# Transposing the first-occurrence counts by DMA from ScalarE's queue, and a select product behind each s product

## The chip, the cores and the metric

One core of a Trainium2 chip. The metric is the device time of one launch in microseconds (us); lower is better. Engines: TensorE (PE), VectorE (DVE), ScalarE (ACT), GpSimd (POOL), and SyncE (SP), which issues all the transfers of the kernel before. TensorE's granted clock was 0.999 of its upper level (2.4 GHz) over the whole profiled execution.

## The reference, cut to what matters

Two layers run on x of shape 4 x 512 x 512 (four chunks of 512 rows). Each layer is `xn = layernorm(x); x = x + s(xn) * silu(g(xn))`. The change touches layer 0's g:

```
inter = xn @ c1_w.T @ c2_w.T                       # [rows, 1792], rank 16
blk   = inter.reshape(rows, 56, 32)                # 56 segments of 32
idx   = argmax(blk, axis=-1) + arange(0, 1792, 32) # first largest in each segment
h     = relu(sum(w1[idx] * xn))                    # one h for each segment
g     = h @ w2t[idx]
```

and layer 0's s is `xn @ (block-masked weight).T + bias`. The kernel computes g densely: h for all 1792 columns, set to zero where the column isn't the first largest of its segment, and then times w2t.

## The kernel before, in words

Float32 products are done as three products of a high and a low part (`three`, L372 to L377), so PE does most of its work in one helper line, L376. Layer 0 handles one chunk after another. A chunk has a head and a body, on PE, DVE and ACT alike.

**Head.** `rank_product` (8 products) gives t, which ACT (L710) and DVE (L901) split. Then come four s products of 12 matmuls each, one for each tile of 128 rows; they alternate between banks 0 and 1, and ACT empties a bank with `s_read` (L716), so that s product tt waits for s_read tt-2. The 1792 columns of `inter` are cut into four pieces, p = 0 to 3 (512, 512, 512 and 256 columns), and each piece has four row tiles tt. For one pair (p, tt), PE computes a select product (L1182) into bank 6, and DVE does three steps, `select`: the largest of each segment (L914, seg_top), equality with it (L916, eq), and a scan that restarts at each segment and counts the equals so far (L926, counts). The row tiles of piece 0 are done in the head, with PE's select tt one s product late: s0, s1, select 0, s2, select 1, s3, select 2; select 3 follows the first up product.

**Body.** `it` runs over the 14 tiles of 128 columns. PE: up product `it` (12 matmuls, h transposed: columns on partitions), one select product of the next piece while it <= 12, `transpose_counts(it - 1)`, and the down product `it - 2` (12 matmuls into banks 2 to 5). `transpose_counts` is four transposes of 128x128 bf16 (L1201) of counts into bank 7, because counts has rows on partitions and h has columns there. ACT: relu of the up product into h (L728; waits for h_lo of the tile before), then h_hi (L737). DVE: a `select` of the next piece, the mask h = (count is 1) * h (L944, reads bank 7), and h_lo (L953). The down product `it` waits for h_lo `it`. Only one relu'd h exists at a time. A new chunk's rows are normalized and transposed at the end of the body (L354, L314, L321, L328).

Counts has room for two pieces of four row tiles. Before its first use, its bytes serve as `c2_rep`, a zeroed tile (L861) in which ACT spreads c2_w (L756) for PE to transpose.

**Startup.** PE, ACT and DVE turn the weights (`items`: PE transposes, ACT `item_hi`, DVE `item_lo`), three items after each s product of chunk 0 (`AFTER_S`). An item's bank is free when item n-5 is split (`w_lo`). The mask of w_s0 goes DVE L884, PE L1258, DVE L889, POOL L639. POOL then splits w2 and later adds the bias and gates.

**SP** issues the loads in its own order; in a chunk it loads the next x_tile and then x_res (1 MB each) once the stores of the chunk before have landed.

Of the kernel before, what the change touches and what calls it, by code (L numbers as in the profile page):

```python
# [6 lines left out]
P = 128  # L7
# [11 lines left out]
def block_mask_ffn_then_attention_lora_kernel(  # L19
# [53 lines left out]
    with ctx:  # L73
# [52 lines left out]
        c1_stack = span_c.take("c1_stack", [P, KD, P], F32R)  # L126
        c1_nat = span_c.take("c1_nat", [RANK, D])
        next_c = Span(span_c.start)
        wqkv_nat = next_c.take("wqkv_nat", [P, KD, 3 * DH])
# [4 lines left out]

        span_s = Span(max(span_c.end, next_c.end, next_c2.end))
        ws_hi = span_s.take("ws_hi", [P, KD, D], F32R)
# [36 lines left out]
        h_lo = span_2.take("h_lo", [P, 2, S], F32R)  # L173
        mask_nat = before_h.take("mask_nat", [P, TT, D], I32)
        rest_2 = Span(span_2.start)
# [45 lines left out]
        mask_on = sem("mask_on")  # L221
        ws0_masked = sem("ws0_masked")
        c2_wide = sem("c2_wide")
        half_bias = sem("half_bias")
# [18 lines left out]
        sel_count = sem("sel_count")  # L243
        first_tr = sem("first_tr")
        up_done = sem("up_done")
# [138 lines left out]
        c2_nat = x_res[:, 0, 0:IT * RANK].rearrange("p (i r) -> p i r", r=RANK)  # L384
        c2_rep = counts[:].bitcast(F32).rearrange("p a t n -> p (a t n)")[:, 0:IT * P]
        c2_rep_q = c2_rep.rearrange("p (i q r) -> p i q r", q=4, r=Q)
# [3 lines left out]
        mask_bank = banks[5]  # L390
        first = banks[7][:].bitcast(BF16)[:, 0:S]
        NSEL = PIECES * TT
# [103 lines left out]
        def item_hi(act, n):  # L496

            kind, i = items[n]
            act.wait_ge(w_tr, n + 1)
            if kind == "c1":  # L500
                act.wait_ge(consts_dve, 12)
# [203 lines left out]
        def _(act):  # L705
# [6 lines left out]
            def s_read(c, tt):  # L712
# [39 lines left out]

            act.wait_ge(consts_dve, 12)
            act.wait_ge(ld_c2, 16)
# [101 lines left out]
        def _(dve):  # L856
# [7 lines left out]
            dve.wait_ge(consts_dve, 6)  # L864
            nc.vector.memset(restart[:].rearrange("p (s n) -> p s n", n=SEG)[:, :, 0:1], 0.0).then_inc(consts_dve, 1)
# [54 lines left out]
            def select_count(c, p, tt):  # L920
                n = p * TT + tt
                dve.wait_ge(sel_eq, c * NSEL + n + 1)
                if tt == 0 and p >= 2:

                    dve.wait_ge(first_tr, c * IT + 4 * (p - 1))
                nc.vector.tensor_tensor_scan(counts[:, p % 2, tt, 0:PW[p]], restart[:, 0:PW[p]], eq[:, 0:PW[p]], 0.0,  # L926
                                             ALU.mult, ALU.add).then_inc(sel_count, 1)

            def head(c):
                t_rest(c)  # L930
                for tt in range(TT - 1):
                    select(c, 0, tt)

            def body(c, last):
                select(c, 0, TT - 1)
                for it in range(IT):
# [39 lines left out]
            for tt in range(TT):  # L976
                if tt:
                    select(0, 0, tt - 1)
                for n in AFTER_S[tt]:
                    item_lo(dve, n)  # L980
            with dve.Fori(0, CH - 1) as c:
                body(c, False)
# [173 lines left out]
        def _(pe):  # L1156
# [37 lines left out]

            def transpose_counts(c, it):

                pe.wait_ge(sel_count, c * NSEL + (it // 4 + 1) * TT)
                if it:
                    pe.wait_ge(h_masked, c * IT + it)
                for tt in range(TT):  # L1200
                    last = nc.tensor.transpose(first[:, rows(tt)], counts[:, it // 4 % 2, tt, rows(it % 4)], ident_bf[:])  # L1201
                last.then_inc(first_tr, 1)

            def down_product(it, tts):
# [7 lines left out]
            def head(c):  # L1212
                pe.wait_ge(xT_done, c * TT + TT)
                rank_product()
                s_product(c, 0)
                s_product(c, 1)
                select(c, 0, 0)
                s_product(c, 2)
                select(c, 0, 1)
                s_product(c, 3)  # L1220
                select(c, 0, 2)

            def body(c, last):
                up_product(c, 0)
                select(c, 0, 3)


                for it in range(1, IT + 1):
# [10 lines left out]
                    transpose_counts(c, it - 1)  # L1239
                    if it >= 2:  # L1240
# [31 lines left out]
            for tt in range(TT):  # L1272
# [3 lines left out]
                for n in AFTER_S[tt]:  # L1276
                    item_in(pe, n)
            with pe.Fori(0, CH - 1) as c:
                body(c, False)
# [192 lines left out]
```

## Time and profile before

| | us |
|---|---|
| median of three runs | 699.52 |
| lowest, highest | 699.08, 701.77 |
| profiled execution, first to last instruction (span) | 697.0 |
| chunk 1 of layer 0, from one rank product to the next (131.36 to 233.53) | 102.2 |
| layer 1 begins at about | 430 |

The profiled execution has no separate total on the page, only its span; the median stands 2.5 us above it, and that difference is what lies around the instructions. Rows of a timeline give start and duration in us, then engine, line, operation, the tile written and the tile read; in square brackets stands the idle time of the engine just before and what ended it. "Issue" rows of SPq are the instructions that start a DMA. Matmul ends are modelled: the distance between starts tells what a product costs.

### The profile page before, as it was taken

What the parts mean: (1) busy time and instruction counts of PE and PEld (TensorE: products, weight loads), DVE (VectorE), ACT (ScalarE), POOL (GpSimd) and SP (SyncE); (2) the same over time, 40 slices, a digit from 0 to 9 for tenths busy, and PEclk for the clock granted to TensorE, in tenths of its full rate; (3) what the DMA queues carried; (4) which work ended last, traced back from release to release, by engine and by line L of the source; (5) the groups of instructions that cost most, each with busy time, mean ns of one, the idle gap of its engine ahead of it and who ended that gap; (6) DMA issues with size and microseconds to landing.
All of it is one profiled execution on the core that took longest, in us unless ns stands there. A gap on an engine that the chain in (4) does not pass through costs nothing.

```text
span 697.0 us, 9078 instructions
## 1 busy us (share of the span) xinstructions
PE 671.0 (96%) x3220; PEld 529.0 (76%) x3220; DVE 457.7 (66%) x741; ACT 208.3 (30%) x371; POOL 204.2 (29%) x175
## 2 busy tenths in 40 slices
PE   4989999999999999999999999889999999999997
PEld 3867777777777777787777787667877887787787
DVE  8798664596765596665686656684855566485543
ACT  2621222412122312222311132563136115313610
POOL 3299100360000550000630003624424242442441
PEclk9999999999999999999999999999999999999999
DMA  8563000040000040000150004530021013002001
GB/s 273 188 189 111 14 1 0 23 159 0 0 0 0 31 149 0 0 0 0 45 197 1 0 1 122 121 136 1 30 91 62 0 46 135 0 30 90 1 15 46
DMA packets 30570, 40.25 MB, mean 58 GB/s; under 512 B 11888, under 2 KB 12656, under 8 KB 30544
## 3 DMA queue, kind: packets, MB, share of 16 engines
q1 hardware_dynamic: 30544, 39.90, 17.5%
q8 instruction: 16, 0.26, 0.2%
q14 instruction: 10, 0.08, 0.0%
HBM read 31.51 MB, written 8.39 MB: 57 GB/s over the span
## 4 chain that ended last, share of the span: by engine, by line
PE 83%; DVE 9%; issue 4%; DMA 1%; ACT 1%; POOL 1%; SPq 0%; DVEq 0%; POOLq 0%
PE bank L376 73%; DVE eq L916 2%; DVE seg_top L914 2%; PE bank L1201 2%; PE bank L314 2%; DVE counts L926 2%; PE bank L1297 2%; DMA s_tile<-in_L_attn_weight 1%; PE bank L1182 1%; PE bank L1334 1%; PE bank L1162 1%; POOL s_tile L639 1%; DVE h_lo L953 1%; DVE w1T_lo L522 1%; DVE x_tile L354 0%
## 5 line engine op out<-in xcount | busy, mean ns | idle before, releaser
L737 ACT ACTIVATE h_hi<-h 128x512 fp32r<-128x512 f32 x56 | 35.4, 632 | 206.6 <-DVE h L944 206.6
L376 PE MATMUL bank<-w_hi_t,h_hi 128*128 128x512 f32 x224 | 93.6, 418 | 0.8 <-DVE h_lo L953 0.6
L914 DVE TENSOR_REDUCE seg_top<-bank 128x16 f32<-128x512 f32 (+1 forms) x64 | 39.5, 617 | 77.2 <-PE bank L1182 77.2
L376 PE MATMUL bank<-xT_hi,w1T_hi 128*128 128x512 f32 x224 | 88.7, 396 | 0.0
L376 PE MATMUL bank<-w_hi_t,h_lo 128*128 128x512 f32 x224 | 88.5, 395 | 0.0
L376 PE MATMUL bank<-w_lo_t,h_hi 128*128 128x512 f32 x224 | 88.5, 395 | 0.0
L376 PE MATMUL bank<-xT_hi,w1T_lo 128*128 128x512 f32 x224 | 88.5, 395 | 0.0
L376 PE MATMUL bank<-xT_lo,w1T_hi 128*128 128x512 f32 x224 | 88.4, 395 | 0.0
L926 DVE TENSOR_TENSOR_SCAN counts<-restart,eq 128x512 bf16<-128x512 bf16 (+1 forms) x64 | 82.1, 1283 | 2.0
L346 POOL TENSOR_TENSOR rstd<-mean_var,eps 128x4 f32<-128x4 f32 x8 | 1.6, 203 | 271.9 <-DVE mean_var L340 271.9
L360 POOL TENSOR_TENSOR g_tile<-g_tile,s_tile 128x512 f32<-128x512 f32 x31 | 40.6, 1311 | 104.9 <-DVE g_tile L970 66.1
L693 POOL TENSOR_TENSOR prod_lo<-prod,prod_hi 128x512 fp32r<-128x512 f32 x32 | 40.7, 1292 | 64.1 <-ACT prod_hi L782 63.9
L953 DVE TENSOR_TENSOR h_lo<-h,h_hi 128x512 fp32r<-128x512 f32 x56 | 41.3, 738 | 27.0 <-ACT h_hi L737 25.4
L376 PE MATMUL bank<-b_hi,prod_hi 128*128 128x512 f32 (+1 forms) x136 | 52.7, 387 | 0.0
L376 PE MATMUL bank<-b_hi,prod_lo 128*128 128x512 f32 (+1 forms) x136 | 51.4, 378 | 0.0
L376 PE MATMUL bank<-b_lo,prod_hi 128*128 128x512 f32 (+1 forms) x136 | 51.3, 377 | 0.0
L728 ACT ACTIVATE h<-bank 128x512 f32<-128x512 f32 x56 | 33.6, 599 | 57.5 <-DVE h_lo L953 48.0
L376 PEld LDWEIGHTS bank<-w_hi_t,h_lo 128*128 128x128 f32 x224 | 42.1, 188 | 10.1
L376 PEld LDWEIGHTS bank<-xT_hi,w1T_lo 128*128 128x128 f32 x224 | 42.0, 188 | 10.0
L376 PEld LDWEIGHTS bank<-xT_lo,w1T_hi 128*128 128x128 f32 x224 | 42.1, 188 | 9.9
L376 PEld LDWEIGHTS bank<-xT_hi,w1T_hi 128*128 128x128 f32 x224 | 42.1, 188 | 9.8
L376 PEld LDWEIGHTS bank<-w_hi_t,h_hi 128*128 128x128 f32 x224 | 42.2, 188 | 8.8 <-DVE h_lo L953 1.4
(201 smaller groups left out, 1327.4 us busy)
## 6 DMA issues: line engine op xcount, KB each, us to landing
x_res<-in_L_attn_data SPq DMA_DIRECT2D x4, 1024.0 KB, 7.6
mid_state<-g_tile SPq DMA_DIRECT2D x16, 256.0 KB, 2.1
x_tile<-mid_state SPq DMA_DIRECT2D x4, 1024.0 KB, 7.5
x_res<-mid_state SPq DMA_DIRECT2D x4, 1024.0 KB, 5.5
out<-g_tile SPq DMA_DIRECT2D x15, 256.0 KB, 2.0
x_tile<-in_L_attn_data SPq DMA_DIRECT2D x3, 1024.0 KB, 5.4
g_tile<-in_L_ffn_w SPq DMA_DIRECT2D x8, 256.0 KB, 5.4
g_tile<-in_L_ffn_w2t SPq DMA_DIRECT2D x8, 256.0 KB, 3.7
```

The costliest lines, as they stand in the source:

```text
L314: last = nc.tensor.transpose(rows_bank(g, tt)[:, k * P:(k + 1) * P], x_tile[:, tt, k * P:(k + 1) * P], ident[:])
L360: nc.gpsimd.tensor_tensor(g_tile[:, tt, :], g_tile[:, tt, :], s_tile[:, tt, :], ALU.mult).then_inc(s_free, 1)
L376: last = nc.tensor.matmul(dst, a, b, start=(start and n == 0), stop=(stop and n == len(mms) - 1))
L693: nc.gpsimd.tensor_tensor(prod_lo[:, kt, :], prod[:, kt % 3, :], prod_hi[:, kt, :].bitcast(F32), ALU.subtract).then_inc(prod_split, 1)
L728: nc.scalar.activation(h[:], up[it % 2][:], ACT.Relu).then_inc(relu_done, 1)
L737: nc.scalar.activation(h_hi[:, it % 2, :], h[:], ACT.Copy).then_inc(h_hi_done, 1)
L914: nc.vector.reduce_max(seg_top[:, 0:segs], got, AX.X).then_inc(seg_max, 1)
L916: nc.vector.tensor_tensor(eq[:, 0:PW[p]].rearrange("p (s n) -> p s n", n=SEG), got, seg_top[:, 0:segs, None].to_broadcast([P, segs, SEG]), ...
L926: nc.vector.tensor_tensor_scan(counts[:, p % 2, tt, 0:PW[p]], restart[:, 0:PW[p]], eq[:, 0:PW[p]], 0.0, ALU.mult, ALU.add).then_inc(sel_co ...
L953: nc.vector.tensor_tensor(h_lo[:, it % 2, :], h[:], h_hi[:, it % 2, :].bitcast(F32), ALU.subtract).then_inc(h_split, 1)
L1201: last = nc.tensor.transpose(first[:, rows(tt)], counts[:, it // 4 % 2, tt, rows(it % 4)], ident_bf[:])
L1297: nc.tensor.matmul(pj[kt % 2][:], pick[:, kt, :], combT[:], start=True, stop=True).then_inc(spread_done, 1)
```

## The change

- Counts are no longer transposed by PE. When a row tile's scan is done, ACT waits for it and issues a DMA transpose from SBUF to SBUF into a new tile `first` (two pieces), with all of the piece's columns at once (128 x 512 or 128 x 256 bf16). There are 16 such DMAs in a chunk. Each row tile has a semaphore for the landing.
- DVE's mask reads `first` instead of bank 7, and at the first tile of each piece waits for the four landings.
- `counts` shrinks to two row tiles. A scan waits until the transpose of the row tile two before has landed.
- ACT's transposes of piece 0 stand in the head behind each s_read; in chunk 0, that of tile tt-1 stands between s_read tt and the three items. In the body, one follows h_hi while it < 12.
- PE's select tt follows s product tt in the head, and select 3 comes before up product 0. DVE's four selects of piece 0 are all in the head.
- `c2_rep` moves onto mask_nat's bytes. So its memset goes from DVE's start to a place behind the wait for `mask_cnt`, ahead of L889.

```diff
-        counts = span_2.take("counts", [P, 2, TT, BANK], BF16)
+        first = span_2.take("first", [P, 2, TT, S], BF16)
...
+            def turn_counts(c, p, tt):
+                act.wait_ge(sel_count, c * NSEL + p * TT + tt + 1)
+                if p >= 2:
+                    act.wait_ge(h_masked, c * IT + 4 * (p - 1))
+                elif not (isinstance(c, int) and c == 0):
+                    act.wait_ge(h_masked, c * IT)
+                act.sem_inc(turns, 1)
+                act.dma_start_transpose(first[:, p % 2, 0:PW[p] // P, rows(tt)], counts[:, tt % 2, 0:PW[p]])\
+                    .then_inc(ld_first[tt], 16)
...
             def head(c):            # ACT
                 t_round(c)
                 for tt in range(TT):
                     s_read(c, tt)
+                    turn_counts(c, 0, tt)
...
                     nc.scalar.activation(h_hi[:, it % 2, :], h[:], ACT.Copy).then_inc(h_hi_done, 1)
+                    if it < 4 * (PIECES - 1):
+                        turn_counts(c, it // 4 + 1, it % 4)
...
             t_round(0)              # ACT, chunk 0
             for tt in range(TT):
                 s_read(0, tt)
+                if tt:
+                    turn_counts(0, 0, tt - 1)
                 for n in AFTER_S[tt]:
                     item_hi(act, n)
+            turn_counts(0, 0, TT - 1)
...
-            nc.vector.memset(c2_rep, 0.0).then_inc(consts_dve, 1)     # DVE's start
...
             dve.wait_ge(mask_cnt, 1)
+            nc.vector.memset(c2_rep, 0.0).then_inc(c2_zero, 1)
             nc.vector.tensor_scalar(on[:, 0:TT * MB], mask_bank[:, 0:TT * MB], 0.0, None, ALU.is_gt).then_inc(mask_on, 1)
...
-                if tt == 0 and p >= 2:
-                    dve.wait_ge(first_tr, c * IT + 4 * (p - 1))
+                turned = c * PIECES + p + (1 if tt >= 2 else 0)
+                if not (isinstance(turned, int) and turned == 0):
+                    dve.wait_ge(ld_first[(tt + 2) % TT], turned * 16)
...
-                    dve.wait_ge(first_tr, c * IT + it + 1)
-                    nc.vector.scalar_tensor_tensor(h[:], first, 1.0, h[:], ALU.is_equal, ALU.mult).then_inc(h_masked, 1)
+                    if it % 4 == 0:
+                        for tt in range(TT):
+                            dve.wait_ge(ld_first[tt], (c * PIECES + it // 4 + 1) * 16)
+                    nc.vector.scalar_tensor_tensor(h[:], first[:, it // 4 % 2, it % 4, :], 1.0, h[:], ALU.is_equal, ALU.mult).then_inc(h_masked, 1)
...
-            def transpose_counts(c, it):     # PE, and its call in the body
...
             def head(c):            # PE
                 pe.wait_ge(xT_done, c * TT + TT)
                 rank_product()
-                s_product(c, 0)
-                s_product(c, 1)
-                select(c, 0, 0)
-                s_product(c, 2)
-                select(c, 0, 1)
-                s_product(c, 3)
-                select(c, 0, 2)
+                for tt in range(TT):
+                    s_product(c, tt)
+                    select(c, 0, tt)
             def body(c, last):
                 up_product(c, 0)
-                select(c, 0, 3)
```

## Rows read from the trace of the kernel before

**Rows 1.** The page: busy time by engine; the chain that ended last, by engine.
```profile
PE 671.0 (96%) x3220; PEld 529.0 (76%) x3220; DVE 457.7 (66%) x741; ACT 208.3 (30%) x371; POOL 204.2 (29%) x175
...
PE 83%; DVE 9%; issue 4%; DMA 1%; ACT 1%; POOL 1%; SPq 0%; DVEq 0%; POOLq 0%
```

**Rows 2.** PE's timeline in one body iteration, from an up product on.
```profile
177.29 0.40 PE L376 MATMUL bank<-xT_hi,w1T_hi 128*128 128x512 f32 x1
...
180.33 0.40 PE L1201 MATMUL bank<-ident_bf,counts 128*128 128x128 bf16 x4
...
180.85 0.40 PE L376 MATMUL bank<-w_lo_t,h_hi 128*128 128x512 f32 x1
```

**Rows 3.** Timeline of ACT and DVE in the next iteration.
```profile
189.24 0.67 DVE L944 SCALAR_TENSOR_TENSOR h<-bank,h 128x512 f32<-128x512 bf16 x1
...
189.94 0.63 ACT L737 ACTIVATE h_hi<-h 128x512 fp32r<-128x512 f32 x1 [4.07 <-DVE h L944]
...
190.61 0.69 DVE L953 TENSOR_TENSOR h_lo<-h,h_hi 128x512 fp32r<-128x512 f32 x1
```

**Rows 4.** Timeline of chunk 1's head: DVE, and PE's first down product.
```profile
139.34 0.69 DVE L914 TENSOR_REDUCE seg_top<-bank 128x16 f32<-128x512 f32 x1 [4.12 <-PE bank L1182]
...
146.38 0.66 DVE L914 TENSOR_REDUCE seg_top<-bank 128x16 f32<-128x512 f32 x1
...
147.80 2.08 DVE L926 TENSOR_TENSOR_SCAN counts<-restart,eq 128x512 bf16<-128x512 bf16 x1
...
153.01 0.69 DVE L944 SCALAR_TENSOR_TENSOR h<-bank,h 128x512 f32<-128x512 bf16 x1 [0.56 <-PE bank L1201]
...
154.94 0.68 DVE L953 TENSOR_TENSOR h_lo<-h,h_hi 128x512 fp32r<-128x512 f32 x1
...
156.03 0.48 PE L376 MATMUL bank<-w_hi_t,h_hi 128*128 128x512 f32 x1
```

**Rows 5.** The page's DMA issues (KB each, us to landing), and an issue from SP's timeline.
```profile
b_nat<-in_L_ffn_B SPq DMA_DIRECT2D x4, 512.0 KB, 7.9
...
out<-g_tile SPq DMA_DIRECT2D x2, 128.0 KB, 1.7
a_nat<-in_L_ffn_A SPq DMA_DIRECT2D x1, 128.0 KB, 3.6
...
146.96 0.41 SPq L568 DMA_DIRECT2D x_tile<-in_L_attn_data  x1
```

**Rows 6.** All instructions on tile b_nat: its DMA issues, durations min/median/max in ns.
```profile
L586 SPq DMA_DIRECT2D b_nat<-in_L_ffn_B x4: 421/2254/4728, 428.2 to 435.6; - x4
```

**Rows 7.** Timeline of the end of chunk 1's body, each engine by itself.
```profile
216.60 0.40 PE L1201 MATMUL bank<-ident_bf,counts 128*128 128x128 bf16 x4
...
222.99 0.69 DVE L944 SCALAR_TENSOR_TENSOR h<-bank,h 128x512 f32<-128x512 bf16 x1 [2.61 <-PE bank L1201]
...
224.98 1.91 DVE L354 TENSOR_SCALAR x_tile<-x_tile,mean_var,rstd 128x512 f32<-128x512 f32 x4
...
219.02 0.63 ACT L737 ACTIVATE h_hi<-h 128x512 fp32r<-128x512 f32 x1 [3.88 <-DVE h L944]
```

**Rows 8.** Timeline of the startup: the memset, an issue, w_s0's mask.
```profile
2.34 1.55 DVE L861 MEMSET counts<- 128x1792 f32 x1 [0.32 <-issue]
...
5.51 0.69 SPq L552 DMA_DIRECT2D x_res<-in_L_ffn_c_w  x1
...
13.33 0.22 DVE L889 TENSOR_SCALAR h<-bank 128x64 f32<-128x64 f32 x1
...
13.79 4.33 POOL L639 TENSOR_TENSOR s_tile<-s_tile,h 128x512 f32<-128x512 f32 x4 [3.45 <-DMA s_tile<-in_L_attn_weight]
```

**Rows 9.** Timeline of chunk 0's head on DVE, from the first scan's end to the first mask.
```profile
33.51 1.26 DVE L522 TENSOR_TENSOR w1T_lo<-bank,w1T_hi 128x512 fp32r<-128x512 f32 x2
...
46.65 2.23 DVE L926 TENSOR_TENSOR_SCAN counts<-restart,eq 128x512 bf16<-128x512 bf16 x1
49.45 0.69 DVE L944 SCALAR_TENSOR_TENSOR h<-bank,h 128x512 f32<-128x512 bf16 x1 [0.57 <-PE bank L1201]
```

More of the change, by code:

```diff
@@ L127, in block_mask_ffn_then_attention_lora_kernel @@
         c1_nat = span_c.take("c1_nat", [RANK, D])
+        counts_at = Span(span_c.start + 4 * KD * 3 * DH)
+        counts = counts_at.take("counts", [P, 2, BANK], BF16)
         next_c = Span(span_c.start)
@@ L133, in block_mask_ffn_then_attention_lora_kernel @@
         prod = next_c2.take("prod", [P, 3, S])
-        span_s = Span(max(span_c.end, next_c.end, next_c2.end))
+        span_s = Span(max(span_c.end, counts_at.end, next_c.end, next_c2.end))
         ws_hi = span_s.take("ws_hi", [P, KD, D], F32R)
@@ L173, in block_mask_ffn_then_attention_lora_kernel @@
         h_lo = span_2.take("h_lo", [P, 2, S], F32R)
-        mask_nat = before_h.take("mask_nat", [P, TT, D], I32)
+        mask_nat = nc.alloc_sbuf_tensor_at("mask_nat", [P, TT, D], I32, offset=before_h.end)
+        c2_rep = before_h.take("c2_rep", [P, TT * D])[:, 0:IT * P]
         rest_2 = Span(span_2.start)
@@ L222, in block_mask_ffn_then_attention_lora_kernel @@
         ws0_masked = sem("ws0_masked")
+        c2_zero = sem("c2_zero")
         c2_wide = sem("c2_wide")
@@ L243, in block_mask_ffn_then_attention_lora_kernel @@
         sel_count = sem("sel_count")
-        first_tr = sem("first_tr")
+        turns = sem("turns")
+        ld_first = [sem(f"ld_first_{tt}") for tt in range(TT)]
         up_done = sem("up_done")
@@ L390, in block_mask_ffn_then_attention_lora_kernel @@
         mask_bank = banks[5]
-        first = banks[7][:].bitcast(BF16)[:, 0:S]
         NSEL = PIECES * TT
@@ L500, in item_hi @@
             if kind == "c1":
-                act.wait_ge(consts_dve, 12)
+                act.wait_ge(consts_dve, 11)
             if kind == "c2":
@@ L751, in _ @@
                 item_hi(act, n)
-            act.wait_ge(consts_dve, 12)
+            act.wait_ge(c2_zero, 1)
             act.wait_ge(ld_c2, 16)
@@ L860, in _ @@
             nc.vector.memset(c1_stack[:].bitcast(F32), 0.0).then_inc(consts_dve, 1)
-            nc.vector.memset(c2_rep, 0.0).then_inc(consts_dve, 1)
             nc.vector.memset(seg_ones, 0.0).then_inc(consts_dve, 1)
             nc.vector.memset(comb[:], 0.0).then_inc(consts_dve, 1)
-            dve.wait_ge(consts_dve, 6)
+            dve.wait_ge(consts_dve, 5)
             nc.vector.memset(restart[:].rearrange("p (s n) -> p s n", n=SEG)[:, :, 0:1], 0.0).then_inc(consts_dve, 1)
@@ L922, in select_count @@
                 dve.wait_ge(sel_eq, c * NSEL + n + 1)
-                if tt == 0 and p >= 2:
-                    dve.wait_ge(first_tr, c * IT + 4 * (p - 1))
-                nc.vector.tensor_tensor_scan(counts[:, p % 2, tt, 0:PW[p]], restart[:, 0:PW[p]], eq[:, 0:PW[p]], 0.0,
+                turned = c * PIECES + p + (1 if tt >= 2 else 0)
+                if not (isinstance(turned, int) and turned == 0):
+                    dve.wait_ge(ld_first[(tt + 2) % TT], turned * 16)
+                nc.vector.tensor_tensor_scan(counts[:, tt % 2, 0:PW[p]], restart[:, 0:PW[p]], eq[:, 0:PW[p]], 0.0,
                                              ALU.mult, ALU.add).then_inc(sel_count, 1)
@@ L930, in head @@
                 t_rest(c)
-                for tt in range(TT - 1):
+                for tt in range(TT):
                     select(c, 0, tt)
             def body(c, last):
-                select(c, 0, TT - 1)
                 for it in range(IT):
@@ L980, in _ @@
                     item_lo(dve, n)
+            select(0, 0, TT - 1)
             with dve.Fori(0, CH - 1) as c:
@@ L1193, in up_product @@
                                       for k in range(KD)]).then_inc(up_done, 1)
-            def transpose_counts(c, it):
[L1197 to L1202, printed above, removed]
             def down_product(it, tts):
@@ L1214, in head @@
                 rank_product()
-                s_product(c, 0)
-                s_product(c, 1)
-                select(c, 0, 0)
-                s_product(c, 2)
-                select(c, 0, 1)
-                s_product(c, 3)
-                select(c, 0, 2)
+                for tt in range(TT):
+                    s_product(c, tt)
+                    select(c, 0, tt)
             def body(c, last):
                 up_product(c, 0)
-                select(c, 0, 3)
                 for it in range(1, IT + 1):
@@ L1238, in body @@
                         transpose_rows(pe, c + 1, 0)
-                    transpose_counts(c, it - 1)
                     if it >= 2:
@@ L1277, in _ @@
                     item_in(pe, n)
+            select(0, 0, TT - 1)
             with pe.Fori(0, CH - 1) as c:
```

1 line of the change is left out of this document (removed).

## The prediction, made before the changed kernel ran

> **What bounds the kernel now.** I read the page first: PE is busy for 96% of the span and makes up 83% of the chain that ended last, DVE 9% [rows 1]. So a PE instruction that goes is worth its whole time wherever PE runs without a gap, and every wait that the change adds matters only where PE ends up waiting for it. Then PE's timeline of one body iteration [rows 2]: from 177.29 to 180.33 PE starts 12 up products and one select product, 0.234 us each, then the four transposes, and the second down product starts at 180.85. The 0.52 us between the last two hold one product (0.234), so the transposes cost 0.29. An iteration is 25 x 0.234 + 0.29 = 6.13 us. Third, ACT and DVE in the next iteration [rows 3]: mask, h_hi and h_lo end at 191.30, and PE's next down product comes at 180.54 + 2 x 6.13 = 192.80, so this chain has 1.5 us to spare. Last come the three places where PE does not run freely: a chunk's head, where DVE's selects end late and PE waits for h_lo [rows 4]; the end of the body [rows 7]; and the startup [rows 8, 9].
>
> **Transposes off PE (gain).** 14 groups in a chunk. Two stand before the first down product, whose start is set by DVE in any case, so 12 count: 12 x 0.29 = 3.5 us in each chunk, 14.0 in four. An iteration becomes 5.84. DVE's mask no longer waits for bank 7.
>
> **The two unknown prices.** No DMA transpose stands in the trace. First x, the time for which its issue holds ACT. Plain issues on SP took 0.41 [rows 5] and 0.69 [rows 8]; the slowest typical one, with its queue full, 2.25 [rows 6]. The transpose is the more complicated form, so I take 0.7, and 0.41 and 2.25 for the ends. Then L, from the issue to the landing of 128 KB. A plain store of 128 KB alone took 1.7, a load of 128 KB amid others 3.6, and 512 KB in runs of 256 bytes, queued, 7.9 [rows 5]. A chunk's head has SP's two loads of 1 MB beside it (one issued at 146.96), so I lean on 3.6 and add the 0.3 by which my x exceeds a plain issue: L = 3.9, ends 1.7 and 7.9. At the end of a body the piece has 256 columns, half the bytes. Between 3.6 for 128 KB and 7.9 for 512 KB lie 1.1 us per 100 KB, so 64 KB less is 0.7: 3.2 there.
>
> ACT itself has room: it idles 4.07 us before each h_hi [rows 3], and x fits there. The three masks in mid-body that wait for a new piece do not bind either: the last issue follows h_hi at 190.57, the next tile's mask is due at 189.24 + 5.84 = 195.08, which hides 4.5 us, and the spare 1.5 - 0.29 = 1.2 makes it 5.7. If L is above that, each such mask costs the excess.
>
> On the issue, the Trainium skill (DMA: Bandwidth & Descriptors, the table in the section on why a DMA increments its semaphore by 16) gives for earlier generations 631 cycles for a small transpose and, from SBUF to SBUF, one command per tile, 262,144 cycles for 8,192 tiles. [...] No row here shows it.
>
> **Chunk heads 1 to 3.** Before, DVE waits until 139.34 for select 0 (idle 4.12), then runs its selects without a gap [rows 4]. Select 0 now comes one s product earlier, 12 x 0.234 = 2.8 us, and all four follow: the fourth seg_top starts at 147.0 instead of 149.8. Its scan starts 1.42 later (146.38 to 147.80), at 148.4. The one before took 2.08 beside POOL's additions, which now cover the fourth too: it ends at 150.5. The landing is at 150.5 + L, the mask starts there, and h_lo ends 2.6 later, as from 153.01 to 155.62 before. PE's first down product starts at 153.15 + L against 156.03: a gain of 2.9 - L, with L = 3.9 a loss of 1.0. The waits of scans 2 and 3 for the landing of the tile two before are covered up to about L = 4.7 (scan 0 ends near 140.3, scan 2 starts near 145.0). s_reads now stand behind a wait for a scan: s product 3 and up products 0 and 1 wait for them, and relu 0 stands behind the fourth issue. PE has products left to do until h_lo, so for x up to about 1.5 this ends before the landing does: nothing.
>
> **End of each body.** The last piece's fourth transpose is issued behind h_hi 11. In the old trace this h_hi ended at 219.65, 3.05 after the transposes of that iteration [rows 7]; PE then has 3 x 12 products, 8.4 us, until the row transposes. These need the mask of tile 12, and then the first of four normalizations: 224.98 + 0.48 - 222.99 = 2.5 us after the mask starts. So PE waits for 3.05 + L + 2.5 - 8.4 = L - 2.85; before, this mask waited 2.6 us for PE instead. With 3.2: 0.4 us, in four chunks 1.6. This wait is what is late next once PE is faster.
>
> **Startup and chunk 0.** The memset of 1.55 us ran at 2.34, while loads were on their way [rows 8]. Now it stands ahead of L889 (13.33), on which POOL's masking of w_s0 waits (13.79), and the items, the s products and all else behind it: +1.5. Then the items: ACT's item_hi now waits for the scan of DVE and an issue, while DVE's item_lo before started at 33.51, right as its scan ended [rows 9]. DVE is without a gap from there to the first mask, so each of the three groups adds x + 0.6 for the copy + 0.1 for semaphores = 1.4: +4.2. Finally the mask: it began 0.57 after the last scan's end (46.65 + 2.23 = 48.88, 49.45), now L: +3.3. Chunk 0: 1.5 + 4.2 + 3.3 - 3.5 = +5.5. Here the cover is gone altogether, since DVE sets the pace.
>
> **Sum.** Chunk 0 +5.5; chunks 1 to 3: 3 x (1.0 - 3.5) = -7.5; ends +1.6: -0.4. Layer 1 has no change. From the span of 697.0 to 696.6, and with the 2.5 us around it, 699.1.
>
> **Rivals.** (1) The transposes are cheap: L = 2.2, x = 0.5. Head: -0.7 - 3.5 = -4.2 each; ends 0; chunk 0: 1.5 + 3.6 + 1.6 - 3.5 = +3.2. Sum -9.4: 690. For it speaks the store of 1.7 [rows 5] and idle DMA engines for most of the body; against it the two big loads in the head. The Trainium skill says as much (Advanced Engine Details and Errata, X-Bar Transpose (TRN2)): transposing DMAs are as fast as regular ones. With that rule the time would be this rival's.
>
> (2) Slower, because the landing is late at every place where PE waits for it: L = 5.5 in the heads and 5.0 at the ends, x = 1.2. Heads 5.5 - 2.9 + 0.8 for the scans that now wait - 3.5 = -0.1 each; ends 2.15 x 4 = +8.6; chunk 0: 1.5 + 5.7 + 4.9 - 3.5 = +8.6. Sum +17: 716. It decides from about L = 4.5 on. The load in small runs speaks for it, x_tile and x_res in the same engines too. The Trainium skill's rule that SP's and ACT's DMAs interleave on the same 16 engines (DMA: Bandwidth & Descriptors, Issuing engines are not separate DMA queues) points the same way.
>
> (3) L at 7.9 or over: the head +5 and some 6 for the scans' waits, three masks at 2.2 each, the end +4.4: some +18 per chunk after the 3.5 are off, about 770. Only the queued load speaks for it.
>
> (4) The issue holds ACT for 2.25, L = 4: chunk 0 1.5 + 8.9 + 3.4 - 3.5 = +10.3, heads 1.1 + 0.7 (up product 1 behind the last s_read) - 3.5 = -1.7 each; ends +1.8: +7, 706.
>
> (5) The change does less than it says: ACT's waits are met early and the ladder of chunk 0 hides, so that only the 14 us and the memset count: 687 to 690. DVE's timeline without a gap speaks against it.
>
> **How the numbers follow.** What a measurement of this kernel can tell from no change is about 0.5%, 3.5 us. The forecast 0.33, rival 1 0.25, rival 2 0.24, rival 3 0.07, rival 4 0.07, rival 5 0.04. Faster is rivals 1 and 5 and the lower edge of the forecast's own range: 0.31. Slower is rivals 2, 3, 4: 0.38. Same 0.31. The forecast alone spans 694 to 704. Each us of L costs 8 (three heads, the mask of chunk 0, four ends) and each us of x 3. With both at their low ends (1.7, 0.41) the sum is -11.7: heads -4.7 each, chunk 0 +2.4. The range takes in rival 1's 690 and rival 2's 716: 689 to 719.
>
> **What would show it.** PE without L1201, and iterations of 5.84 us. DVE's mask at a chunk's first tile idle and released by the DMA, 3 to 4 us after the last scan. PE's first down product released by h_lo, at about 157 on the old clock where it was 156.03. Row transposes of the next chunk waiting for DVE L354. POOL's L639 at 15.3. DVE idle about 1.4 us before each of three item groups. I'd be wrong if the landing took under 2.5 or over 5 us, or if PE lost time in mid-body.

## The result, and the profile after

The changed kernel takes 717.96 us (median of 5 runs, 714.30 to 719.22), the kernel before 700.21 beside it: a ratio of 1.0244, 95% interval 1.0217 to 1.0271. It is 17.75 us slower, where no change was forecast. The profiled execution has a span of 712.5 us against 697.0, so 15.5 of this stand in its trace. It is the fastest of the five; the others have spans of 716.0 to 717.4 us and granted clocks of 0.978 to 0.981 where it has 0.984, and there is no trace of them.

The page of the changed kernel: PE's busy time, the chain by engine, the mask's group (with its idle time and what ended it), and the queue of the transposes (packets, MB, share of 16 engines).

```profile
PE 666.9 (94%) x2996; PEld 526.6 (74%) x2996; DVE 460.5 (65%) x741; ACT 207.9 (29%) x371; POOL 205.8 (29%) x175
...
q10 hardware_dynamic: 30720, 7.35, 5.1%
...
PE 77%; DVE 11%; DMA 4%; issue 4%; ACT 2%; ACTq 1%; SPq 0%; DVEq 0%
...
L965 DVE SCALAR_TENSOR_TENSOR h<-first,h 128x512 f32<-128x512 bf16 x56 | 38.9, 694 | 28.2 <-DMA first<-counts 28.2
```

Against [rows 1], PE is busy for only 4.1 us less, though its transposes are gone, and its share fell from 96 to 94%. The DMA part of the chain went from 1% to 4%, 3% of it on tile `first`. DVE's mask now idles 28.2 us in all, all of it for the transposes' landing. 30,720 packets for 64 transposes are 480 each on average, of some 240 bytes.

All transposes by their line: durations of the issue in ns, and the time to landing.

```profile
L729 ACTq DMA_TRANSPOSE first<-counts x64: 1184/1206/1320, 36.1 to 437.9; - x64
...
DMA to landing us min/median/max: 2.3/2.4/8.0
```

So x, the time for which an issue holds ACT, is 1.21 us, and L, from issue to landing, is 2.4 in the median, but 8.0 at most. Where the long ones stand decides everything. The windows from one rank product to the next, chunks 1 and 2, and chunk 3 up to layer 1's first product (the row of a window: length, busy time and instructions of PE, PEld, DVE, ACT and POOL, then PE's clock, the DMA share and GB/s):

```profile
139.91:243.53 103.62, 99.36 (x425) 78.49 (x425) 68.62 (x97) 24.45 (x41) 19.76 (x14) 0.98 0.18 48
243.53:345.85 102.32, 98.38 (x425) 77.46 (x425) 68.64 (x97) 24.45 (x41) 19.84 (x14) 1.00 0.17 49
345.85:455.40 109.55, 101.81 (x428) 80.28 (x429) 73.02 (x99) 26.13 (x43) 24.63 (x18) 0.95 0.34 86
```

Before, these were 102.17, 102.14 and 104.43 long. The differences add up: chunk 0 with the startup +8.55 (chunk 1's rank product starts at 139.91, before at 131.36), then +1.45, +0.18, +5.12: +15.3 at the start of layer 1. The forecast had chunks 1 to 3 shorter by 2.5 each, with 0.4 given back at each end.

Mid-body, PE, from down product to down product (against [rows 2]):

```profile
175.69 0.39 PE L381 MATMUL bank<-w_hi_t,h_hi 128*128 128x512 f32 x1
...
181.51 0.39 PE L381 MATMUL bank<-w_hi_t,h_hi 128*128 128x512 f32 x1
```

5.82 us for 25 products without a gap, against 6.13: the gain in the body is there. It is lost in the head. DVE, ACT, SP and PE in chunk 1's head, each engine's timeline by itself:

```profile
157.13 2.06 DVE L946 TENSOR_TENSOR_SCAN counts<-restart,eq 128x512 bf16<-128x512 bf16 x1
165.97 0.69 DVE L965 SCALAR_TENSOR_TENSOR h<-first,h 128x512 f32<-128x512 bf16 x1 [6.78 <-DMA first<-counts]
...
167.30 0.69 DVE L936 TENSOR_TENSOR eq<-bank,seg_top 128x512 bf16<-128x512 f32 x1
167.91 0.68 DVE L974 TENSOR_TENSOR h_lo<-h,h_hi 128x512 fp32r<-128x512 f32 x1
...
155.91 1.21 ACTq L729 DMA_TRANSPOSE first<-counts  x1
...
159.31 1.32 ACTq L729 DMA_TRANSPOSE first<-counts  x1
...
156.40 0.41 SPq L571 DMA_DIRECT2D x_tile<-in_L_attn_data  x1
157.04 0.40 SPq L576 DMA_DIRECT2D x_res<-in_L_attn_data  x1
...
168.04 0.79 PE L1204 MATMUL bank<-c_stack,t_stack 128*128 128x512 f32 x1 [3.25 <-DVE eq L936]
168.64 0.79 PE L381 MATMUL bank<-w_hi_t,h_hi 128*128 128x512 f32 x1
...
170.51 0.63 PE L381 MATMUL bank<-w_lo_t,h_hi 128*128 128x512 f32 x1
170.94 0.48 PE L381 MATMUL bank<-w_hi_t,h_lo 128*128 128x512 f32 x1
171.26 0.39 PE L381 MATMUL bank<-w_hi_t,h_hi 128*128 128x512 f32 x1
```

The reader is to see three things against [rows 4]. The fourth scan ends at 159.19, 19.3 us after the chunk's rank product, where it was 21.1 before: the new order works. The transpose issued at 159.31 lands only at 165.85, beside two loads of 1 MB that were issued 2.9 and 2.3 us ahead of it (that these make it late is shown by the first two experiments). And after PE's wait of 3.25 us its products start 0.43 us apart instead of 0.233, which is the clock's lower level (1.2 GHz), until 171.26. From 168.64 on, six products take 2.62 us instead of 1.40, which costs a further 1.2.

Chunk 3's head is the worst, with the load of wqkv beside it as well (SP, DVE and PE):

```profile
361.96 0.40 SPq L571 DMA_DIRECT2D x_tile<-mid_state  x1
362.49 0.43 SPq L576 DMA_DIRECT2D x_res<-in_L_attn_data  x1
362.95 0.54 SPq L580 DMA_DIRECT2D wqkv_nat<-in_L_attn_Wqkv  x1
...
373.38 0.69 DVE L965 SCALAR_TENSOR_TENSOR h<-first,h 128x512 f32<-128x512 bf16 x1 [8.25 <-DMA first<-counts]
...
375.45 0.80 PE L1204 MATMUL bank<-c_stack,t_stack 128*128 128x512 f32 x1 [5.08 <-DVE eq L936]
```

In all three heads the fourth transpose lands within half a us of the last load issued ahead of it: x_res at 157.04 + 8.4 = 165.4 against 165.85, x_res at 260.61 + 7.7 = 268.3 against 268.8, and wqkv at 362.95 + 10.6 = 373.6 against 373.3.

The third transposes add to this. Chunk 1's was issued at 155.91, half a us ahead of x_tile's load, and still took 6.5 us: it landed at 162.4, as that load did (156.40 + 5.8 = 162.2). In chunk 2 it was the same (265.7 against 265.5). The issue of the transpose ended at 157.12 and that of the load at 156.81, so the order in which the issues end fits here, and the order in which they start doesn't. Chunk 3's third transpose fits neither: it landed at 369.3, between x_tile (367.5) and x_res (371.0).

Chunk 0 on DVE (against [rows 9]), and the startup's memset and POOL's masking (against [rows 8]):

```profile
38.11 1.29 DVE L525 TENSOR_TENSOR w1T_lo<-bank,w1T_hi 128x512 fp32r<-128x512 f32 x2 [2.08 <-ACT w1T_hi L510]
...
45.74 1.29 DVE L525 TENSOR_TENSOR w1T_lo<-bank,w1T_hi 128x512 fp32r<-128x512 f32 x2 [2.02 <-ACT w1T_hi L510]
...
52.35 1.29 DVE L525 TENSOR_TENSOR w1T_lo<-bank,w1T_hi 128x512 fp32r<-128x512 f32 x2 [2.02 <-ACT w1T_hi L510]
...
60.31 0.95 DVE L965 SCALAR_TENSOR_TENSOR h<-first,h 128x512 f32<-128x512 bf16 x1 [3.29 <-DMA first<-counts]
...
13.37 1.55 DVE L908 MEMSET c_rep<- 128x1792 f32 x1 [0.32 <-issue]
...
15.08 4.47 POOL L642 TENSOR_TENSOR s_tile<-s_tile,h 128x512 f32<-128x512 f32 x4 [4.76 <-DVE h L909]
```

DVE idles 6.1 us in the three gaps in front of its item groups (4.2 predicted), and 3.3 ahead of the mask where it was 0.57.

### The profile page after: what moved, and what is told of

Its sections match the earlier page's. It is cut to its first block, busy times and chain, and to the rows that moved or that the text cites. A ratio compares the mean times of both kernels' runs of the same rounds, so it can differ in the third digit from the quotient of the medians.

```text
span 712.5 us, 8775 instructions
## 1 busy us (share of the span) xinstructions
PE 666.9 (94%) x2996; PEld 526.6 (74%) x2996; DVE 460.5 (65%) x741; ACT 207.9 (29%) x371; POOL 205.8 (29%) x175
## 3 DMA queue, kind: packets, MB, share of 16 engines
q10 hardware_dynamic: 30720, 7.35, 5.1%
## 4 chain that ended last, share of the span: by engine, by line
PE 77%; DVE 11%; DMA 4%; issue 4%; ACT 2%; ACTq 1%; SPq 0%; DVEq 0%
PE bank L381 69%; DMA first<-counts 3%; DVE counts L946 2%; DVE seg_top L934 2%; DVE eq L936 2%; PE bank L319 2%; PE bank L1305 1%; PE bank L1204 1%; PE bank L1342 1%; DMA mask_nat<-in_L_attn_mask 1%; DVE x_tile L359 1%; PE bank L1184 1%; ACTq L729 1%; DVE h L965 1%; DVE w1T_lo L525 1%
## 5 line engine op out<-in xcount | busy, mean ns | idle before, releaser
L381 PE MATMUL bank<-xT_hi,w1T_hi 128*128 128x512 f32 x224 | 90.7, 405 | 4.8 <-ACT h L743 2.9
L381 PE MATMUL bank<-w_hi_t,h_hi 128*128 128x512 f32 x224 | 91.8, 410 | 1.6 <-DVE h_lo L974 1.5
L381 PE MATMUL bank<-w_lo_t,h_hi 128*128 128x512 f32 x224 | 90.0, 402 | 0.0
L965 DVE SCALAR_TENSOR_TENSOR h<-first,h 128x512 f32<-128x512 bf16 x56 | 38.9, 694 | 28.2 <-DMA first<-counts 28.2
L974 DVE TENSOR_TENSOR h_lo<-h,h_hi 128x512 fp32r<-128x512 f32 x56 | 39.5, 705 | 26.9 <-ACT h_hi L752 25.4
```

Source lines behind the costliest of these rows:

```text
L381: last = nc.tensor.matmul(dst, a, b, start=(start and n == 0), stop=(stop and n == len(mms) - 1))
L965: nc.vector.scalar_tensor_tensor(h[:], first[:, it // 4 % 2, it % 4, :], 1.0, h[:], ALU.is_equal, ALU.mult).then_inc(h_masked, 1)
L974: nc.vector.tensor_tensor(h_lo[:, it % 2, :], h[:], h_hi[:, it % 2, :].bitcast(F32), ALU.subtract).then_inc(h_split, 1)
```

## The experiments

| kernel | us, median (lowest to highest, runs) | before beside it | ratio, 95% interval |
|---|---|---|---|
| e1_loads_late | 701.12 (699.16 to 702.47, 10) | 700.38 | 1.0016, 1.0000 to 1.0032 |
| e2_memset_later | 717.97 (716.09 to 719.28, 4) | 700.38 | 1.0267, 1.0234 to 1.0299 |
| e3_items_first | 717.10 (714.38 to 718.76, 4) | 700.38 | 1.0259, 1.0230 to 1.0288 |
| e4_all_three | 698.03 (696.29 to 700.73, 10) | 700.38 | 0.9973, 0.9952 to 0.9995 |
| e1b_xres_late | 703.21 (700.61 to 704.53, 10) | 700.11 | 1.0036, 1.0022 to 1.0050 |
| e6_order_alone | 697.28 (695.76 to 699.01, 10) | 700.11 | 0.9959, 0.9943 to 0.9976 |
| e7_small_loads_late | 695.44 (694.58 to 696.16, 4) | 700.11 | 0.9929, 0.9903 to 0.9955 |
| e8_reads_first | 695.96 (694.37 to 697.13, 7) | 700.11 | 0.9934, 0.9912 to 0.9957 |
| e9_ladder_back | 701.39 (699.63 to 702.95, 10) | 700.42 | 1.0012, 0.9997 to 1.0027 |
| e10_half_memset | 693.38 (690.92 to 695.18, 4) | 700.42 | 0.9885, 0.9859 to 0.9910 |
| e7_again | 696.11 (693.82 to 697.80, 9) | 700.48 | 0.9938, 0.9917 to 0.9960 |
| e12_wqkv_later | 694.28 (692.41 to 695.62, 6) | 700.48 | 0.9919, 0.9896 to 0.9941 |

**The loads behind the transposes.** One wait on SP, so that a chunk's loads follow the landing of its fourth transpose; nothing else differs from the changed kernel.

```diff
                 sp.wait_ge(xT_tr, c * TT + TT)
+                sp.wait_ge(ld_first[TT - 1], (c * PIECES + 1) * 16)
                 sp.dma_start(x_tile[:], source)
```

> The changed kernel, but SP issues a chunk's two 1 MB loads (x_tile, x_res) only after the fourth transpose of piece 0 of that chunk has landed. Theory A (in the heads of chunks 1 to 3 the fourth transpose takes 6.5, 5.9 and 8.0 us because it shares the DMA engines with those loads; alone it takes 2.4): the mask's idle time there falls from 6 to 8 us to about 2.5, PE has no wait of 3 us before the first down product and no stretch of half-rate products behind it, and the time falls by 4.1 + 3.5 + 5.6 = 13 us for the landings and up to 3 more for the products at the lower clock: about 702 to 705 where the changed kernel takes 718. Theory B (the head is late because ACT's s_reads and relu stand behind the waits for scans and 1.2 us issues): the landings get shorter but the time falls by less than 4 us.

DVE and SP in chunk 1's head, PE there, the window of chunk 1, and DVE later in chunk 3:

```profile
162.81 0.69 DVE L966 SCALAR_TENSOR_TENSOR h<-first,h 128x512 f32<-128x512 bf16 x1 [2.70 <-DMA first<-counts]
...
162.84 0.41 SPq L572 DMA_DIRECT2D x_tile<-in_L_attn_data  x1
...
159.07 0.50 PE L381 MATMUL bank<-xT_hi,w1T_hi 128*128 128x512 f32 x1 [0.66 <-ACT s_tile L720]
...
140.84:239.75 98.91, 97.82 (x425) 77.50 (x425) 68.64 (x97) 24.47 (x41) 19.77 (x14) 1.00 0.19 51
...
373.33 1.22 DVE L947 TENSOR_TENSOR_SCAN counts<-restart,eq 128x512 bf16<-128x512 bf16 x1 [1.98 <-DMA first<-counts]
```

16.8 us come back from one wait. The mask idles 2.70 instead of 6.78, the clock stays at its upper level (1.00), and a chunk takes 98.91 where it took 103.62. The last row is the price: in chunk 3 the loads that were moved meet piece 1's transposes (one took 8.7 us to land). This shows theory A: in the heads of chunks 1 to 3, L was made long by SP's loads, and PE's long waits and its stretch at the lower clock level came with it. Two things then cancel nearly: chunks 1 and 2 are each 3.3 us shorter than in the kernel before, and the startup with chunk 0 is still 9.5 longer (chunk 1's rank product starts at 140.84, before at 131.36).

**x_res alone late**, to see how far the one load ahead of the transposes counts (the wait stands in front of x_res instead of x_tile).

```diff
                 sp.wait_ge(c2_wide, 1)
+                sp.wait_ge(ld_first[TT - 1], (c * PIECES + 1) * 16)
                 sp.dma_start(x_res[:], x_rows[c])
```

> The changed kernel with only x_res (and what SP issues behind it) moved behind the fourth landing; x_tile's 1 MB load stays where it is, 2.9 us before that transpose's issue. If a transpose waits for what is queued on the DMA engines ahead of it, it lands when x_tile does, 3 to 3.5 us after its issue instead of 6.5: the heads gain 3 + 2.6 + 4.7 us and the time falls to 705 to 708, between e1 (701) and the changed kernel (718). If one load in flight is enough for the full delay: 715 or more.

SP, ACT and DVE in chunk 1's head:

```profile
158.09 0.41 SPq L571 DMA_DIRECT2D x_tile<-in_L_attn_data  x1
...
161.02 1.21 ACTq L730 DMA_TRANSPOSE first<-counts  x1
...
164.44 0.69 DVE L966 SCALAR_TENSOR_TENSOR h<-first,h 128x512 f32<-128x512 bf16 x1 [3.55 <-DMA first<-counts]
```

L = 3.3. The load took 5.7 us to land, till 163.8; the transpose followed at 164.3. The pattern holds with one load ahead as with two or three. The time, 703.21, is better than the 705 to 708 expected.

**The memset behind L909**, so that w_s0's mask does not stand behind it.

```diff
-            nc.vector.memset(c2_rep, 0.0).then_inc(c2_zero, 1)
             nc.vector.tensor_scalar(on[...], mask_bank[...], 0.0, None, ALU.is_gt).then_inc(mask_on, 1)
+            nc.vector.memset(c2_rep, 0.0).then_inc(c2_zero, 1)
```

> The changed kernel, but DVE's memset of c2_rep stands behind L909 (the comparison that lets POOL mask w_s0) instead of ahead of it. If the memset delays the whole startup, as in the prediction's step of +1.5 us: POOL's masking starts at 13.6 to 13.8 instead of 15.08 and the time falls by 1.3 us, 0.2%, or by up to 0.4 less since the memset then delays the first row transposes. If the startup is set by the ladder of chunk 0's scans and item copies alone, nothing changes.

POOL in the startup:

```profile
14.85 6.10 POOL L642 TENSOR_TENSOR s_tile<-s_tile,h 128x512 f32<-128x512 f32 x4 [3.06 <-DMA s_tile<-in_L_attn_weight]
```

No gain, where 1.3 us had been expected. POOL starts earlier with respect to DVE's first reading of the mask (3.48 us behind it instead of 5.23), but with DVE's memset beside it its four instructions take 6.10 us instead of 4.47, and they end 9.6 us behind that reading instead of 9.7. The memset costs the same, on either side.

**Items before the transpose's wait in chunk 0.**

```diff
-                if tt:
-                    turn_counts(0, 0, tt - 1)
                 for n in AFTER_S[tt]:
                     item_hi(act, n)
+                if tt:
+                    turn_counts(0, 0, tt - 1)
```

> The changed kernel, but in chunk 0 ACT copies its three items before it waits for the scan and issues the transpose. If each of the three item groups costs DVE a gap of the issue 1.25 + copy 0.6 + 0.1 = 1.95 us: DVE's three waits for ACT L510 of about 2 us go and the time falls by 5 to 6 us (712), perhaps 1 to 2 more because PE's wait of 5.8 us at 48.99 and the half-rate products behind it go too. If ACT's order does not matter there (DVE and POOL set the pace): under 1 us.

SP and DVE at the end of chunk 0's head:

```profile
52.91 0.58 SPq L563 DMA_DIRECT2D bias_b<-in_L_ffn_base_b  x1
...
58.27 0.95 DVE L965 SCALAR_TENSOR_TENSOR h<-first,h 128x512 f32<-128x512 bf16 x1 [5.76 <-DMA first<-counts]
```

The gaps are gone and the fourth scan ends at 52.5 instead of 57.0. But the transpose that follows it then stands among SP's loads. It was issued at 52.61 and took 5.5 us where it was 3.1; bias_b's load, issued at 52.91 while the transpose's own issue ran, landed at 57.4 and the transpose at 58.1. So the mask starts only 2.0 us earlier: a faster engine moved its transfer into traffic. The time shows less still: 717.10 against 717.96, and no gain with each against the kernel before beside it (1.0259 and 1.0244). One reason is in the trace. In chunk 2's head PE waited for 2.71 us in both kernels, and ran at the lower level behind it here but not in the changed kernel: from the first down product on, six products took 2.7 us here and 1.5 there, and chunk 2 took 104.4 us instead of 102.3. The wait in the changed kernel and here:

```profile
270.97 0.49 PE L1204 MATMUL bank<-c_stack,t_stack 128*128 128x512 f32 x1 [2.71 <-DVE eq L936]
...
269.62 0.80 PE L1204 MATMUL bank<-c_stack,t_stack 128*128 128x512 f32 x1 [2.71 <-DVE eq L936]
```

**All three edits together.**

> All three edits at once. If they are three independent losses, the gains add: 13 to 16 + 1 + 5 to 7 us, which gives 694 to 699, at or below the 700 of the kernel before; the 12 x 4 iterations at 0.29 to 0.31 us less are then what is left. If one hides another, 703 or more.

698.03: the first of them that beats the kernel before. DVE still waits 6.10 us for chunk 0's fourth transpose, issued from 51.76 to 53.01 and landed at 57.6, now beside four small loads for layer 1, issued from 50.98 to 52.68. The last two of these landed at 57.5 and 57.8:

```profile
57.76 0.69 DVE L966 SCALAR_TENSOR_TENSOR h<-first,h 128x512 f32<-128x512 bf16 x1 [6.10 <-DMA first<-counts]
```

**Those four small loads late as well** (on top of the last).

```diff
+            sp.wait_ge(ld_first[TT - 1], 16)
             sp.dma_start(a_nat[R:R + E, :], router_w)
```

> e4 with one edit more: SP issues its four small loads for layer 1 (router_w, lora_a, base_b broadcast to all partitions, bqkv in 4-byte pieces) only after chunk 0's fourth transpose has landed. In e4 that transpose, issued at 51.8, took 6.0 us beside them, and DVE's first mask waited 6.1 us. If small and scattered transfers in flight hold a transpose up as the 1 MB loads do, it lands in 2.4 to 3 us, DVE's wait falls to about 2.6, and the time falls by 3 to 3.5 us: about 694.5 to 695. If it is w2's last loads or POOL's work at that moment, nothing changes.

DVE's first mask:

```profile
54.86 1.48 DVE L967 SCALAR_TENSOR_TENSOR h<-first,h 128x512 f32<-128x512 bf16 x1 [2.78 <-DMA first<-counts]
```

L is 2.5 now. 2.6 us are gained in the medians, 2.9 in this row: small loads hold a transpose just as large ones do.

**The order alone**: the kernel before with the new order of the select products and DVE's selects, PE still transposing.

> The kernel before (counts transposed by TensorE) with the change's second part alone: select tt behind s product tt, and all four selects of piece 0 in the head. If the new order ends the fourth scan 1.9 us earlier (150.5 on the old clock) and PE's two waits before the first down product (0.24 and 1.0 us) go, each of chunks 1 to 3 is 1.2 us shorter: 3.7 us in all, about 696.7. If the order buys nothing without the DMA: 700.

```profile
133.64:234.53 100.89, 100.89 (x480) 79.82 (x480) 67.53 (x97) 24.52 (x41) 20.16 (x14) 1.00 0.09 31
```

That window is its chunk 1: 1.28 us shorter than before, PE without any gap. So 2.8 us of the final gain are the order's. The DMA transposes add 1.98 per chunk on top (98.91 in e1_loads_late), not the 3.5 that leave PE. PE idles 1.1 us of that chunk (98.91 long, 97.82 busy), and not for a landing: it waits 0.66 us for the last s_read (the row shown there), which ACT does behind the third transpose's issue, and twice 0.18 for a relu. Its first down product starts without a gap at 165.68, when h_lo had ended at 165.42.

**The reads of s before the waits** (on top of e7_small_loads_late; in the heads the transpose of tile tt-1 stands behind s_read tt).

```diff
-                    turn_counts(c, 0, tt)
+                    if tt:
+                        turn_counts(c, 0, tt - 1)
+                turn_counts(c, 0, TT - 1)
```

> e7, and in the heads of chunks 1 to 3 ACT empties s product tt+1 before it waits for scan tt and issues its transpose. If the issue of 1.2 us and ACT's order cost the head something of their own (PE waited 0.63 us for an s_read and 0.28 for a relu in the changed kernel), a chunk becomes 0.5 to 0.9 us shorter than e7's (98.9 in e1) and the time falls by 1.5 to 2.7 us. If h_lo alone sets the head: under 0.3 us.

PE in chunk 1's head:

```profile
157.50 0.50 PE L381 MATMUL bank<-xT_hi,w1T_hi 128*128 128x512 f32 x1 [1.26 <-ACT h L747]
```

A miss: 695.96 against 695.44, chunk 1 at 98.94. PE's wait for s_read vanishes, and 1.26 us appear in front of up product 2, which waits for relu 0; on ACT this relu stands behind the fourth transpose's issue. As in e1_loads_late, PE never waits for h_lo in this head. So the order of the reads buys nothing, and the reason is not the expected one: with the loads out of the way the fourth scan, the issue of 1.21 us behind it and the relu set the head's end, and a landing of 2.4 us is hidden.

**The ladder and the early memset back**, with the loads as in e7_small_loads_late: the price of these two by themselves.

> The changed kernel with all of SP's loads moved out of the way (as e1 and e7), but with the memset and chunk 0's order on ACT (scan wait and issue ahead of the three item copies) as in the change. e3 gained only 0.9 us, which fits two theories. If the order costs 3 x 1.95 = 5 to 6 us, and e3 gave it back because its earlier transpose met the loads (5.7 us to land instead of 3.1): this kernel is 5 to 6 us slower than e7's 695.4, some 701. If that order costs next to nothing: 695 to 697.

6.0 us more (701.39 against 695.44; 5.6 with each against the kernel before beside it). The early memset is worth nothing by e2_memset_later, so this is the ladder of chunk 0, DVE's waits for ACT in front of the three item groups: 6.1 us in the changed kernel's trace.

**Half the memset** (only the columns that stay zero).

```diff
-            nc.vector.memset(c2_rep, 0.0)
+            nc.vector.memset(c2_rep_q[:, :, :, RANK:Q], 0.0)
```

> e7, with the memset cut to the half of c2_rep's columns that no copy fills (896 of 1792 to a partition). If the memset is on the path of the startup at its full 1.55 us, the time falls by 0.7 to 0.8 us, to 694.7 (at the edge of what three rounds tell), and POOL's masking, 6.1 us beside the whole memset in e2 and 4.5 without it, falls to about 5.2.

693.38, some 2.1 below e7_small_loads_late, where 0.8 was expected. POOL's masking takes 5.17 instead of 5.97. Two more runs were made for it, on one chip: the kernel of e7_small_loads_late again, and the half memset with wqkv's load (and bias_a's, which follows it) moved behind piece 1's transposes.

```diff
                     sp.wait_ge(t_done, CH)
+                    sp.wait_ge(ld_first[TT - 1], (c * PIECES + 2) * 16)
                     sp.dma_start(wqkv_nat[:], ...)
```

> The kernel of e7_small_loads_late again, beside the one with half the memset on the same chip, because the two were 2.1 us apart (695.44, 693.38) in comparisons of different chips, where the memset's own 0.75 us accounts for less. Theory A (the half memset gives back twice: 0.75 us of VectorE and 0.8 us by which GpSimd's masking, 5.17 against 5.97 us, is less slowed beside it): this one is 1.5 to 2 us slower than the half one. Theory B (only the memset's time counts, the rest was chips and landings): 0.8 us slower.

> The kernel of e10_half_memset and one thing more: in chunk 3 the load of wqkv (and behind it bias_a's) waits until piece 1's four transposes have landed, as x_tile and x_res wait for piece 0's. Against the kernel without it (693.4). Theory A (what is left of the loads' price is the 0.73 us that TensorE waits for h_lo before piece 1's first select in chunk 3, while the scan waits 1.9 us for the transpose that went beside the loads of x_tile, x_res and wqkv, 8.6 us from issue to landing): with a third of those bytes gone the transpose lands in some 6 us and TensorE waits nothing there: 0.7 us faster, 692.7; so 2.2 us or more below the kernel with the whole memset on this chip. Theory B (x_tile and x_res alone hold the transpose): no change, 693.4, and the wait of 0.7 us stays.

They are 1.8 us apart (696.11 and 694.28), for both edits together. PE in chunk 3 with wqkv as it was (e7_again):

```profile
371.11 0.50 PE L381 MATMUL bank<-w_hi_t,h_hi 128*128 128x512 f32 x1 [0.82 <-DVE h_lo L976]
...
432.05 0.66 PE L319 MATMUL bank<-ident,x_tile 128*128 128x128 f32 x4 [1.96 <-DVE xT_lo L333]
433.95 0.60 PE L319 MATMUL bank<-ident,x_tile 128*128 128x128 f32 x4
```

and with wqkv later (e12_wqkv_later), where the first of the three has no counterpart:

```profile
428.80 0.66 PE L319 MATMUL bank<-ident,x_tile 128*128 128x128 f32 x4 [1.95 <-DVE xT_lo L333]
431.73 1.06 PE L319 MATMUL bank<-ident,x_tile 128*128 128x128 f32 x4
```

The wait of 0.82 went, as theory A of that run had it, but chunk 3 took no less (103.0 against 102.7): after the same wait of 1.95 us later on, PE ran at the lower level in one execution (2.93 between the two rows) and not in the other (1.90). PE's idle time in chunk 3 fell from 3.66 to 2.76 us, and its busy time rose from 99.01 to 100.25. So the wait was worth 0.9 in the trace, and wqkv's share of the medians can't be told. From DVE's first reading of the mask to POOL's last masking instruction, 9.59 us pass in the traces of e7_small_loads_late and e7_again, and 8.65 in those of the two kernels with half of it; the rest of the 1.8 to 2.1 us, and how the 0.94 splits between DVE and POOL, stays open. The best version is the one with half the memset, 693.38 (ratio 0.9885): 7 us faster than before, some 25 faster than the change as made.

## Why the prediction was wrong

**Transposes off PE: right.** 0.31 an iteration against 0.29, and 5.82 against 5.84.

**x: too low.** 1.21 against 0.7; I had gone by the plain issues [rows 5, 8], and rival 2's 1.2 was right. The Trainium skill's table (DMA: Bandwidth & Descriptors, the section on why a DMA increments its semaphore by 16) has a transpose within SBUF cost one command per tile in earlier generations. The trace doesn't agree: 128 x 256 has half the tiles of 128 x 512, and its issue takes 1.18 us against 1.21.

**L in the heads: the step that failed.** I took 3.9 by the load of 128 KB amid others [rows 5]; it measured 6.54, 5.85 and 8.00 in the heads of chunks 1, 2 and 3. Alone it is 2.4, near rival 1's 2.2. My value between "alone" and "queued" fits neither. The formula around it roughly held: L - 2.9 - 3.5 with L = 6.54 would have made chunk 1 +0.1 instead of -2.5, and with the 1.2 us of the clock +1.3; measured +1.45. Chunk 2: 5.85 gives -0.55, its products were not slowed, and measured is +0.2. Chunk 3: +1.6 from L, 1.6 from the clock, which stayed low for eight products, and most of the rest of the 5.1 stands at the layer boundary. There, from the last select product of 256 columns on, 20.16 us pass to layer 1's first product instead of 19.36, although its iterations are shorter. PE waits 1.96 us for xT_lo, where before it waited 0.96 for x_tile and 0.84 for xT_lo, and behind this wait it runs at the lower level once more:

```profile
450.11 0.66 PE L319 MATMUL bank<-ident,x_tile 128*128 128x128 f32 x4 [1.96 <-DVE xT_lo L333]
...
455.43 0.39 PE L381 MATMUL bank<-xT_hi,a_hi 128*80 128x512 f32 x1
```

The same stretch of work took 3.9 us before (436.24 to 440.14) and takes 5.3 here, 1.4 more. The cause of the loss in the heads is shown by e1_loads_late and e1b_xres_late. The Trainium skill's rule that DMAs of different engines interleave on the same 16 (DMA: Bandwidth & Descriptors, Issuing engines are not separate DMA queues) agrees, with 2.4 us alone and 5.85 to 8.0 beside SP's loads; I gave it to rival 2 and should have given it to the forecast. The Trainium skill's other rule, that transposing DMAs are as fast as regular ones (Advanced Engine Details and Errata, X-Bar Transpose (TRN2)), holds only roughly: alone, 2.4 against the plain store's 1.7. Beside these loads no run has a plain transfer of 128 KB to compare.

**The clock: not foreseen.** The sum has no term for it. Waits of 3.25 and 5.08 us in the heads cost PE a further 1.2 and 1.6 at the lower level, and the one of 1.96 at the layer boundary 1.4. The trace of before, at 0.999 over the whole execution, had no such wait in the body.

**Ends: too high by the same L.** DVE in the tail of chunk 1's body (against [rows 7]):

```profile
232.66 0.69 DVE L965 SCALAR_TENSOR_TENSOR h<-first,h 128x512 f32<-128x512 bf16 x1 [1.27 <-DMA first<-counts]
```

L was 2.3, no load being beside it; L - 2.85 is then below zero, and PE waited for nothing at the end of chunk 1. 0.4 a chunk was taken, 0 measured. Rival 2 came close in time (716), but that was luck: half of its 17 us stood here.

**Chunk 0.** +5.5 taken, +8.55 measured. The memset: 1.5 taken, 1.55 its row and 1.8 from the mask's landing to POOL's end. The ladder: 4.2 taken, 6.1 measured; x was 0.5 too low each time. The mask: +3.3 taken, +2.7 measured. With the 3.5 off these make 7.1; the other 1.4 us are not assigned. (PE waits 0.92 us for a relu and 0.99 for h_lo in the next two iterations, at 67.66 and 71.96, where no such waits stood before; that they are the 1.4 isn't shown.) The places were all right, so the mechanism stands here and the size of x was off.

**The whole.** Between the forecast's -0.4 and the trace's +15.5 lie 15.9 us: 8.7 of L in the heads (6.54 + 5.85 + 8.00 - 3 x 3.9), 4.2 of the clock, 3.1 of chunk 0, less 1.6 of the ends. The other 1.5 are not assigned.

**Rivals.** Rival 5 fell with DVE's gaps, 3 with the median of 2.4, 4 with the issue's 1.21. A time near the forecast came out only once the loads had been moved (701.12 in e1_loads_late, against 699.1). There one more step of the prediction fails: ACT's waits in the heads were put at nothing because PE has products left until h_lo, which held only while the landing was long; with it at 2.4 they are all that PE waits for (0.66 and twice 0.18 us in chunk 1).

## What to carry to other kernels

A transfer on the critical path is priced by what other queues issued in the few us ahead of it, or while its own issue ran, not by its own size: find those issues in SP's timeline first, and ask what they are needed for; a wait of one semaphore on them gave back 16.8 of 17.75 us. When an engine is made faster or a gap is closed, look where its transfers now fall (in e3_items_first the scan ended 4.5 us earlier and the mask began only 2.0 earlier). And a wait put into an in-order engine's stream (ACT's here) is paid by whatever stands behind it: move the items ahead of it, and look at what is then behind it (the relu in e8_reads_first).

## What the runs showed of the hardware

- A DMA transpose from SBUF to SBUF holds the issuing ACT queue for 1.21 us (128 x 512 bf16) or 1.18 (128 x 256). With no load in flight it lands in 2.4 to 2.6 us and in 2.3 to 2.4.
- Beside loads it lands with the last load whose issue ended before its own did. The distance was at most 0.6 us in the fourth transposes of the changed kernel's chunks 1 to 3, the third of its chunks 1 and 2, and the fourth of chunk 1 in e1b_xres_late and of chunk 0 in e4_all_three (L 3.3 to 8.0), even where the loads are small ones (5.9). The third transpose of the changed kernel's chunk 3 did not fit.
- After a wait of 3.25 us PE's products are 0.43 us apart for six, after one of 5.08 us for eight, and then 0.233 again. After a wait of 2.71 us in the same place this happened in e3_items_first and not in the changed kernel, and after waits of 1.95 us in e12_wqkv_later and not in e7_again: the length of the wait alone doesn't decide it.
- DVE's memset of 1.55 us beside POOL's masking makes this take 6.10 us instead of 4.47, and half the memset 5.17.
